# Turning the cross scores of a graph network's first phase on VectorE and GpSimd in place of TensorE

## The chip, the core and the metric

One core of a Trainium2 chip runs the whole program. Its engines are named as in the profile: PE is TensorE (matmuls), PEld its weight loads, DVE is VectorE, ACT is ScalarE, POOL is GpSimd, SP is the engine that issues the DMAs. Each works through its own queue in order and waits on semaphores. The metric is the device time of one execution in microseconds, the median over runs; lower is better.

## The reference

128 graphs of 64 nodes with 384 features pass through three graph layers. The first two follow each other after one normalisation, the third has a normalisation of its own; a sum with the earlier x closes each block. What a layer computes:

```python
h = jnp.maximum(_layernorm(x, axis=-1), 0.0)             # before layers 1 and 3

u = jnp.einsum('bid,bjd->bij', h, h) / temper            # temper = sqrt(384)
a = jax.nn.softmax(u, axis=-1)
delta = a * adjacency_matrix
attn = delta / (jnp.sum(delta, axis=-1, keepdims=True) + 1e-10)
hl = h @ wl.T + b_l
hs = h @ ws.T + b_s
hr = h @ wr.T + b_r
ctx = (attn * upper) @ hl + diag_a[..., None] * hs + (attn * lower) @ hr
o = (ctx - mean) / jnp.sqrt(var + LN_EPS) * g + beta
h = jax.nn.relu(o)
```

## The kernel before, in words

**Tiles.** Two graphs make a tile of 128 rows, so there are 64 tiles; a step works on two tiles (k = 0 and 1). A phase is one layer, 32 steps, so there are 96 steps (`Step.n`). The body of a step is written for each engine by hand, in the order in which the engine is to run it; a hardware loop (`walk`) repeats it in pairs, with the first two and last four steps of each phase written out. In the body for step s, PE projects and weighs the tiles of s while everything else prepares s+1 (`nxt`), up to the normalisation of s+4 (`fourth`).

**Precision.** PE multiplies rounded fp32 numbers. To keep fp32 accuracy each operand is split into a rounded part HI (made by ACT) and the rest LO (made by DVE), and a product is three matmuls: HI·HI, HI·LO, LO·HI. For the scores both operands are the same nodes, so LO·HI is the transpose of HI·LO. `scores` therefore makes, for each tile, 128 columns of HI·HI and 128 columns of HI·LO in one PSUM bank (`score_bank`, seen as `scores4` [row, tile, which of the two, column]). The second block is called the cross scores.

**The transposed part before.** ACT copies the cross scores of both tiles to SBUF (`copy_cross`, L548). PE multiplies each tile's copy by the identity (`turn_cross`, L426), which adds its transpose onto HI·HI in PSUM. DVE adds the copy itself (`sum_scores`, L744): two instructions, one for each half of the partitions, since of a tile of two graphs only the two 64x64 blocks on the diagonal are wanted. Then come the exponentials (ACT, L565), `mask_edges` (DVE, L773), `place_edges` (POOL, L989 and L993).

**The order of a step on PE.** Projection RIGHT of tile 0, `weigh` of the previous step's tile 1 (L475, six matmuls: three with the RIGHT side parts, then three with the LEFT ones), projection LEFT of tile 0, projection SELF of tile 0 (L442, nine matmuls each), `scores` of the next step (L418), projection RIGHT of tile 1, `turn_cross` of the next step, `weigh` of tile 0, projections LEFT and SELF of tile 1. I call the `weigh` of tile 1, which runs in the step after, the second `weigh`.

**What else the prediction names.** DVE: `split_nodes` (L727, the LO part of the next step's nodes), `context_stats` (L813), `split_side` (L808, the LO part of a projection), `turn_nodes` (L723, a transpose of 128x768 in 32x32 squares, for the tiles three steps ahead), `gather_input` (L710 and L711, mean and variance of the rows four steps ahead), `centre` (L832), `norm` (L841). ACT: `split_side` (L589), `fill_source` (L532), which waits for `split_nodes` on DVE. POOL: `input_rstd` (L977, L979), which waits for both `gather_input`, and `output_rstd` (L983).

```python
for side in (RIGHT, LEFT):
    pe.wait_ge(side_hi[side], s.tile(k) + 1)
    pe.wait_ge(side_lo[side], s.tile(k) + 1)
    for a, b in PASSES:
```

## Time and profile before

| | |
|---|---|
| median of 3 runs | 1239.68 us (1238.2 to 1240.05) |
| profiled execution | 1238.95 us |
| its span | 1237.2 us |
| PE busy | 98% |
| DVE busy | 88% |
| ACT busy | 67% |
| POOL busy | 26% |
| two products of `turn_cross` (L426) | 192 matmuls, 96 pairs, 32 of them in the first phase |

How to read the rows further down. A timeline row is: start in us, length in us, engine, line of the kernel, operation, tile written <- tiles read, shape, count; in brackets how long the engine was idle just before and what ended that. Instructions in one row are merged, so its length is that of all of them. Rows of one engine can overlap: an instruction may begin before the one ahead of it has fully ended. Matmul ends are modelled, so the distance between the starts of two PE rows says more than a length. A row of a stretch gives, for PE, PEld, DVE, ACT and POOL in this order, the busy time and the number of instructions, then the granted PE clock, the DMA share and GB/s. A row of a group is: line, engine, operation, tiles, shapes, count | busy us, mean ns of one | idle before it and what ended that.

### The profile page before, as it was taken

Reading aid. Unit: us, or ns where it says so; the run is one execution under the profiler, and the core shown is the slowest. Engines: PE = TensorE matmul, PEld = TensorE weight load, DVE = VectorE, ACT = ScalarE, POOL = GpSimd, SP = SyncE. Lnnn points to the kernel's source line nnn. Section 1 sums busy time; section 2 is a strip of 40 time slices with the busy share of each in tenths; the row PEclk is TensorE's granted clock in tenths of the full one; section 3 lists DMA queues with packets and bytes.
Section 4 is the critical chain, followed back from the end, with each engine's and each line's share of the span. In section 5 each row is a group of like instructions: output and inputs, shape, how many; then the busy total and the mean of one; then the engine's idle time right before and its main releaser. Section 6 shows DMA issues by size and latency. Waiting matters only on the chain.

```text
span 1237.2 us, 27493 instructions
## 1 busy us (share of the span) xinstructions
PE 1218.6 (98%) x7162; PEld 1209.0 (98%) x7162; DVE 1090.4 (88%) x3125; ACT 833.8 (67%) x2079; POOL 324.4 (26%) x438
## 2 busy tenths in 40 slices
PE   8899999999999999999999999999999999999997
PEld 6899999999999999999999999999999999999997
DVE  6888888888887889999999999999999999999986
ACT  5666666666667776666667666776666666666663
POOL 2322222222223321111212121342323232323221
PEclk9899999999999999999999999999999999999999
DMA  5423232323233333233333333432232323232321
GB/s 178 134 82 119 83 119 83 117 84 115 87 106 122 106 100 103 95 101 100 95 106 95 106 95 106 133 108 95 96 106 95 106 95 102 97 97 97 99 96 43
DMA packets 112899, 126.91 MB, mean 103 GB/s; under 512 B 11104, under 2 KB 100192, under 8 KB 112864
## 3 DMA queue, kind: packets, MB, share of 16 engines
q1 hardware_dynamic: 112864, 126.50, 32.7%
q8 instruction: 15, 0.25, 0.1%
q14 instruction: 20, 0.16, 0.0%
HBM read 76.91 MB, written 49.55 MB: 102 GB/s over the span
## 4 chain that ended last, share of the span: by engine, by line
PE 92%; DVE 4%; issue 3%; POOL 1%; ACT 0%; POOLq 0%; DVEq 0%; ACTq 0%
PE left_bank L442 23%; PE right_bank L442 23%; PE context_bank L442 23%; PE context_bank L475 16%; PE score_bank L418 5%; PE score_bank L426 1%; DVE node_t L727 1%; DVE context L841 0%; POOL weight L1000 0%; DVE weight L796 0%; DVE in_stats L706 0%; DVE turned L723 0%; DVE context L832 0%; PE right_bank L499 0%; DVE attn_t L801 0%
## 5 line engine op out<-in xcount | busy, mean ns | idle before, releaser
L442 PE MATMUL left_bank<-weight,node_t 128*128 128x384 f32 x1728 | 338.9, 339 | 0.3 <-DVE weight L796 0.3
L442 PE MATMUL context_bank<-weight,node_t 128*128 128x384 f32 x1728 | 333.1, 337 | 1.9 <-DVE weight L796 1.9
L442 PE MATMUL right_bank<-weight,node_t 128*128 128x384 f32 x1728 | 333.7, 337 | 0.6 <-ACT right_bank L583 0.6
L589 ACT ACTIVATE side_parts<-right_bank 128x384 fp32r<-128x384 f32 x192 | 94.4, 491 | 316.6 <-PE context_bank L475 316.6
L442 PEld LDWEIGHTS context_bank<-weight,node_t 128*128 128x128 f32 x1728 | 304.2, 189 | 2.4 <-issue 2.2
L442 PEld LDWEIGHTS left_bank<-weight,node_t 128*128 128x128 f32 x1728 | 305.3, 189 | 0.6 <-issue 0.6
L442 PEld LDWEIGHTS right_bank<-weight,node_t 128*128 128x128 f32 x1728 | 298.7, 188 | 1.4 <-issue 1.1
L475 PE MATMUL context_bank<-side_parts,attn_t 128*128 128x386 f32 x1152 | 241.5, 345 | 5.7 <-issue 5.4
L475 PEld LDWEIGHTS context_bank<-side_parts,attn_t 128*128 128x128 f32 x1152 | 199.8, 190 | 8.5 <-issue 7.5
L727 DVE TENSOR_TENSOR node_t<-nodes,node_t 128x768 fp32r<-128x768 f32 x94 | 120.4, 1281 | 17.7 <-ACT node_t L537 17.6
L993 POOL TENSOR_TENSOR edge_block<-edge,tri 128x512 f32<-128x512 f32 x96 | 133.7, 1393 | 0.0
L983 POOL TENSOR_TENSOR rstd<-spread,scalars 128x2 f32<-128x2 f32 x96 | 66.2, 689 | 257.0 <-DVE spread L824 257.0
L723 DVE STREAM_TRANSPOSE turned<-nodes 128x768 f32<-128x768 f32 x94 | 92.0, 979 | 45.7 <-ACT nodes L532 42.7
L601 ACT ACTIVATE context_bank<-context_bank,diag 128x386 f32<-128x386 f32 x192 | 105.1, 547 | 36.9 <-PE context_bank L442 36.1
L989 POOL TENSOR_TENSOR own_edge<-edge,tri 128x128 f32<-128x128 f32 x96 | 47.3, 493 | 302.7 <-DVE edge L773 302.7
L832 DVE SCALAR_TENSOR_TENSOR context<-context_bank,moments,vector_rows 128x384 f32<-128x384 f32 x192 | 117.1, 610 | 2.4
L813 DVE BATCH_NORM_STATS2 stats<-context_bank 128x6 f32<-128x384 f32 x192 | 107.3, 559 | 11.9 <-PE context_bank L475 11.9
L808 DVE TENSOR_TENSOR side_parts<-right_bank,side_parts 128x384 fp32r<-128x384 f32 x192 | 106.7, 556 | 10.9 <-ACT side_parts L589 7.0
L808 DVE TENSOR_TENSOR side_parts<-left_bank,side_parts 128x384 fp32r<-128x384 f32 x192 | 103.0, 536 | 1.6 <-ACT side_parts L589 1.6
L977 POOL TENSOR_TENSOR in_spread<-in_moments,scalars 128x2 f32<-128x2 f32 x64 | 17.3, 271 | 312.5 <-DVE in_moments L711 312.5
L595 ACT ACTIVATE context_bank<-vector_rows 128x386 f32<-128x386 f32 x192 | 94.5, 492 | 0.0
L583 ACT ACTIVATE left_bank<-vector_rows 128x384 f32<-128x384 f32 x192 | 93.7, 488 | 0.0
(75 smaller groups left out, 1521.5 us busy)
## 6 DMA issues: line engine op xcount, KB each, us to landing
squares<-turned SPq DMA_DIRECT2D x94, 384.0 KB, 2.7
nodes<-squares SPq DMA_DIRECT2D x376, 96.0 KB, 2.2
rows<-x SPq DMA_DIRECT2D x64, 384.0 KB, 3.6
out<-rows SPq DMA_DIRECT2D x31, 384.0 KB, 2.6
adj_in<-adj SPq DMA_DIRECT2D x96, 64.0 KB, 1.9
piece<-weights SPq DMA_DIRECT2D x18, 192.0 KB, 2.6
rows<-weights SPq DMA_DIRECT2D x3, 576.0 KB, 8.0
vector_rows<-vectors SPq DMA_DIRECT2D x3, 384.0 KB, 7.0
```

What stands on the lines that cost most here:

```text
L442: mm = nc.tensor.matmul(bank[:, 0:D], node_t[:, s.parity, k, c, a], weight[:, s.phase % 2, w, c, b], start=False, stop=(c, a) == (CH - 1, ...
L475: mm = nc.tensor.matmul(context_bank[k][:, 0:DX], attn_t[:, a, k, 1 - side], side_parts[:, side, b], start=False, stop=(side == LEFT and a ...
L583: nc.scalar.activation(side_bank[side][k][:, 0:D], vector_row(s.phase, ROW_LEFT + side), ACT.Copy)\
L589: nc.scalar.activation(side_parts[:, side, HI, 0:D], side_bank[side][k][:, 0:D], ACT.Copy).then_inc(side_hi[side], 1)
L595: nc.scalar.activation(context_bank[k][:, 0:DX], vector_row(s.phase, ROW_SELF, 2), ACT.Copy)\
L601: nc.scalar.activation(context_bank[k][:, 0:DX], context_bank[k][:, 0:DX], ACT.Identity, scale=diag[:, s.parity, k:k + 1]).then_inc(self_s ...
L723: nc.vector.transpose(turned[:, :, :], source_blocks).then_inc(nodes_turned, 1)
L727: nc.vector.tensor_tensor(node_rows(s, LO), moved_rows, node_rows(s, HI).bitcast(F32), ALU.subtract).then_inc(node_lo, 1)
L808: nc.vector.tensor_tensor(side_parts[:, side, LO, 0:D], side_bank[side][k][:, 0:D], side_parts[:, side, HI, 0:D].bitcast(F32), ALU.subtrac ...
L813: nc.vector.bn_stats(stats[:, k], context_bank[k][:, 0:D]).then_inc(stats_done, 1)
L832: nc.vector.scalar_tensor_tensor(context[:, k], context_bank[k][:, 0:D], moments[:, k, 0:1], vector_row(s.phase, ROW_GAMMA), ALU.subtract, ...
L993: nc.gpsimd.tensor_tensor(edge_block[:, :, :, :].rearrange("p k u (h j) -> p k (u h) j", h=2), edge[:, :, :].unsqueeze(2).to_broadcast([P, ...
```

## The change

Only steps of the first phase (n below 32) are treated in the new way (`squared`); in the other two phases the code does what it did.

- PE: the two products with the identity are gone, at the start as well.
- ACT: the copy of the cross scores is two instructions of 64 partitions, each only of the 64 columns for each tile that are wanted.
- DVE: `turn_cross` reads the cross scores in PSUM. Two transposes of 64x128 turn every 32x32 square in place; then, after a wait of DVE on its own result, four transposes of 32x64 write the off-diagonal squares of each 64x64 block over it, each to the neighbouring quarter of the partitions. They go to `own_edge`, a buffer that is free at that time.
- POOL: `add_cross` adds ACT's copy onto the turned squares.
- DVE: `sum_scores` waits for POOL and adds the result to HI·HI.

DVE, second step of the program (the body of a step, written out), from the input statistics to the second `norm`. Before:

```order
L706 BN_STATS in_stats<-rows 128x6 x2
L841 SCALAR_TENSOR_TENSOR rows<-context,rstd,vector_rows 128x384
L744 TENSOR_TENSOR score<-score_bank,cross 64x128 x2
L710 MEMSET scalars 128x1
L711 BN_AGGR in_moments<-in_stats 128x2
L710 MEMSET scalars 128x1
L711 BN_AGGR in_moments<-in_stats 128x2
L808 TENSOR_TENSOR side_parts<-right_bank,side_parts 128x384
L841 SCALAR_TENSOR_TENSOR rows<-context,rstd,vector_rows 128x384
```

The same place on DVE now; L866 is `norm`, L833 `split_side`, L770 the sum:

```order
L866 SCALAR_TENSOR_TENSOR rows<-context,rstd,vector_rows 128x384
L753 STREAM_TRANSPOSE own_edge<-score_bank 64x128 x2
L758 STREAM_TRANSPOSE own_edge<-score_bank 32x2x32 x4
L719 MEMSET scalars 128x1
L720 BN_AGGR in_moments<-in_stats 128x2
L719 MEMSET scalars 128x1
L720 BN_AGGR in_moments<-in_stats 128x2
L833 TENSOR_TENSOR side_parts<-right_bank,side_parts 128x384
L770 TENSOR_TENSOR score<-score_bank,own_edge 64x128 x2
L866 SCALAR_TENSOR_TENSOR rows<-context,rstd,vector_rows 128x384
```

Where the sum stood there are six transposes; the sum has moved behind both gathers and the RIGHT `split_side`.

POOL, the same step, from `output_rstd` to `place_edges`. Before:

```order
L983 TENSOR_TENSOR rstd<-spread,scalars 128x2
L977 TENSOR_TENSOR in_spread<-in_moments,scalars 128x2
L979 TENSOR_TENSOR in_rstd<-in_spread,scalars 128x2
L1000 TENSOR_TENSOR weight<-piece,weight 128x384 x2
L989 TENSOR_TENSOR own_edge<-edge,tri 128x128
```

The same place on POOL now; L1015 is the new addition:

```order
L1019 TENSOR_TENSOR rstd<-spread,scalars 128x2
L1008 TENSOR_TENSOR in_spread<-in_moments,scalars 128x2
L1010 TENSOR_TENSOR in_rstd<-in_spread,scalars 128x2
L1015 TENSOR_TENSOR own_edge<-own_edge,cross 128x128
L1036 TENSOR_TENSOR weight<-piece,weight 128x384 x2
L1025 TENSOR_TENSOR own_edge<-edge,tri 128x128
```

The addition stands behind the two operations of `input_rstd`, which need DVE's gathered moments.

```diff
@@ -70,6 +70,8 @@
         self.phase = self.n // PAIRS if isinstance(half, int) else phase
         self.g = self.n - PAIRS * self.phase
         self.bounded = self.phase != 1
+
+        self.squared = self.phase == 0
 
         self.normal = self.n - (PAIRS if self.phase == 2 else 0)
 
@@ -192,6 +194,8 @@
         first_bank = [edge_bank, score_bank]
         max_rows = edge_bank[:, 0:2 * NODES].rearrange("p (k i) -> p k i", k=2)
         score_copy = cross[:, :, 0:NODES]
+        cross_upper = cross[:, 0, :].rearrange("p (k j) -> p k j", k=2)
+        cross_lower = own_edge[:, :, :]
         scores4 = score_bank[:, :].rearrange("p (k a j) -> p k a j", k=2, a=2)
         source = nodes[:, :].rearrange("p (k d) -> p k d", k=2)
         source_blocks = nodes[:, :].rearrange("p (n q y) -> p q n y", q=QUARTERS, y=Q)
@@ -421,7 +428,7 @@
 
             def turn_cross(s):
 
-                pe.wait_ge(cross_copied, s.n + 1)
+                pe.wait_ge(cross_copied, 2 * s.n + 2)
                 for k in range(2):
                     mm = nc.tensor.matmul(score_bank[:, k * 256:k * 256 + P], cross[:, k], ident_r[:, :],
                                           start=False, stop=True, skip_group_check=True)
@@ -488,7 +495,7 @@
                 if nxt.exists():
                     scores(nxt)
                 project_side(s, 1, RIGHT)
-                if nxt.exists():
+                if nxt.exists() and not nxt.squared:
                     turn_cross(nxt)
                 weigh(s, 0)
                 project_side(s, 1, LEFT, within=(lambda: spread_max(nxt)) if nxt.exists() and not nxt.bounded else None)
@@ -509,8 +516,6 @@
             start = Step(0, 0, 0)
             transpose_first(start)
             scores(start)
-            open_bank(edge_bank)
-            turn_cross(start)
             walk(pe, body)
             weigh(Step(2, STEPS // 2 - 1, 1), 1)
 
@@ -545,7 +550,11 @@
             def copy_cross(s):
                 act.wait_ge(scored, s.n + 1)
                 at_least(act, score_summed, 2 * s.n)
-                nc.scalar.activation(cross[:, :, :], scores4[:, :, 1, :], ACT.Copy).then_inc(cross_copied, 1)
+                if not s.squared:
+                    nc.scalar.activation(cross[:, :, :], scores4[:, :, 1, :], ACT.Copy).then_inc(cross_copied, 2)
+                    return
+                for h, half in enumerate(HALVES):
+                    nc.scalar.activation(cross_upper[half], scores4[half, :, 1, h * NODES:(h + 1) * NODES], ACT.Copy).then_inc(cross_copied, 1)
 
             def totals(s):
                 act.wait_ge(max_bias_done, s.n + 1 - PAIRS)
@@ -737,13 +746,29 @@
                                                  node_t[:, s.parity, k, :, HI].bitcast(F32), ALU.subtract)
                 mm.then_inc(node_lo, 1)
 
+            def turn_cross(s):
+
+                dve.wait_ge(cross_copied, 2 * s.n + 2)
+                for h, half in enumerate(HALVES):
+                    mm = nc.vector.transpose(cross_lower[half], scores4[half, :, 1, h * NODES:(h + 1) * NODES])
+                mm.then_inc(squares_turned, 1)
+                dve.wait_ge(squares_turned, s.n + 1)
+                for q in range(QUARTERS):
+                    to, side, at = q ^ 1, q % 2, q // 2 * NODES
+                    mm = nc.vector.transpose(cross_lower[to * Q:(to + 1) * Q, :, side * Q:(side + 1) * Q],
+                                             scores4[q * Q:(q + 1) * Q, :, 1, at + (1 - side) * Q:at + (2 - side) * Q])
+                mm.then_inc(lower_turned, 1)
+
             def sum_scores(s):
 
-                dve.wait_ge(cross_turned, s.n + 1)
+                if s.squared:
+                    dve.wait_ge(cross_added, s.n + 1)
+                else:
+                    dve.wait_ge(cross_turned, s.n + 1 - PAIRS)
                 for h, half in enumerate(HALVES):
+                    other = cross_lower[half] if s.squared else cross[half, :, h * NODES:(h + 1) * NODES].bitcast(F32)
                     nc.vector.tensor_tensor(score[half], scores4[half, :, 0, h * NODES:(h + 1) * NODES],
-                                            cross[half, :, h * NODES:(h + 1) * NODES].bitcast(F32),
-                                            ALU.add).then_inc(score_summed, 1)
+                                            other, ALU.add).then_inc(score_summed, 1)
 
             def row_maximum(s):
 
@@ -863,8 +888,9 @@
                 split_side(s, 0, LEFT)
                 split_edges(s)
                 input_shift(second)
+                turn_cross(nxt)
+                turn_nodes(second)
                 sum_scores(nxt)
-                turn_nodes(second)
                 split_side(s, 1, RIGHT)
                 gather_stats(third)
                 context_stats(s, 0)
@@ -904,7 +930,9 @@
                     input_stats(fourth, 1)
                 if prev.exists():
                     norm(prev, 0)
-                if nxt.exists():
+                if nxt.exists() and nxt.squared:
+                    turn_cross(nxt)
+                if nxt.exists() and not nxt.squared:
                     sum_scores(nxt)
                 if nxt.exists() and not nxt.bounded:
                     row_maximum(nxt)
@@ -915,6 +943,8 @@
                 if prev.exists() and prev.phase > 0:
                     residual(prev, 0)
                 split_side(s, 1, RIGHT)
+                if nxt.exists() and nxt.squared:
+                    sum_scores(nxt)
                 if prev.exists():
                     norm(prev, 1)
                 context_stats(s, 0)
@@ -952,6 +982,7 @@
             input_shift(start.ahead(1))
             split_first(RIGHT)
             split_first(LEFT)
+            turn_cross(start)
             sum_scores(start)
             mask_edges(start)
             split_first(SELF)
@@ -978,6 +1009,11 @@
                 pool.wait_ge(in_spread_done, s.normal + 1)
                 nc.gpsimd.tensor_tensor(in_rstd[:, :], in_spread[:, :], minus_half[:, :], ALU.pow).then_inc(in_rstd_done, 1)
 
+            def add_cross(s):
+
+                pool.wait_ge(lower_turned, s.n + 1)
+                nc.gpsimd.tensor_tensor(cross_lower, cross_lower, cross_upper.bitcast(F32), ALU.add).then_inc(cross_added, 1)
+
             def output_rstd(s):
                 pool.wait_ge(spread_done, s.n + 1)
                 nc.gpsimd.tensor_tensor(rstd[:, :], spread[:, :], minus_half[:, :], ALU.pow).then_inc(rstd_done, 1)
@@ -1002,6 +1038,7 @@
 
             def first_step(s):
                 input_rstd(s.ahead(2))
+                add_cross(s.ahead(1))
                 input_rstd(s.ahead(3))
                 place_edges(s.ahead(1))
                 input_rstd(s.ahead(4))
@@ -1015,6 +1052,8 @@
                     output_rstd(prev)
                 if fourth.exists() and fourth.bounded:
                     input_rstd(fourth)
+                if nxt.exists() and nxt.squared:
+                    add_cross(nxt)
                 if len(pieces) > 0:
                     split_piece(*pieces[0])
                 if len(pieces) > 1:
@@ -1027,6 +1066,7 @@
             input_rstd(start)
             input_rstd(start.ahead(1))
             pool.wait_ge(triangles_in, 16)
+            add_cross(start)
             place_edges(start)
             walk(pool, body)
             output_rstd(Step(2, STEPS // 2 - 1, 1))
```

## Rows read from the trace of the kernel before

**Rows 1.** The page: busy time of the engines; chain that ended last.

```profile
PE 1218.6 (98%) x7162; PEld 1209.0 (98%) x7162; DVE 1090.4 (88%) x3125; ACT 833.8 (67%) x2079; POOL 324.4 (26%) x438
...
PE 92%; DVE 4%; issue 3%; POOL 1%; ACT 0%; POOLq 0%; DVEq 0%; ACTq 0%
```

**Rows 2.** Busy time of each engine from 100 to 399 us.

```profile
100.00:399.00 299.00, 299.00 (x1777) 299.00 (x1776) 248.69 (x754) 204.71 (x507) 79.60 (x119) 1.00 0.34 102
```

**Rows 3.** Timeline of PE, one step of the first phase.

```profile
212.11 1.21 PE L475 MATMUL context_bank<-side_parts,attn_t 128*128 128x386 f32 x6
213.16 1.74 PE L442 MATMUL left_bank<-weight,node_t 128*128 128x384 f32 x9
...
218.58 0.33 PE L426 MATMUL score_bank<-ident_r,cross 128*128 128x128 f32 x2
218.75 1.28 PE L475 MATMUL context_bank<-side_parts,attn_t 128*128 128x386 f32 x6
219.87 1.74 PE L442 MATMUL left_bank<-weight,node_t 128*128 128x384 f32 x9
...
224.57 0.68 PE L475 MATMUL context_bank<-side_parts,attn_t 128*128 128x386 f32 x3
```

**Rows 4.** Timeline of DVE, the same step.

```profile
210.77 0.55 DVE L808 TENSOR_TENSOR side_parts<-left_bank,side_parts 128x384 fp32r<-128x384 f32 x1
...
212.09 0.96 DVE L727 TENSOR_TENSOR node_t<-nodes,node_t 128x768 fp32r<-128x768 f32 x1 [0.58 <-ACT node_t L537]
213.35 0.57 DVE L813 BATCH_NORM_STATS2 stats<-context_bank 128x6 f32<-128x384 f32 x1 [0.30 <-PE context_bank L475]
...
215.65 0.98 DVE L723 STREAM_TRANSPOSE turned<-nodes 128x768 f32<-128x768 f32 x1 [0.75 <-ACT nodes L532]
...
219.56 0.60 DVE L744 TENSOR_TENSOR score<-score_bank,cross 64x128 f32<-64x128 f32 x2
220.22 0.06 DVE L710 MEMSET scalars<- 128x1 f32 x1
...
220.65 0.56 DVE L808 TENSOR_TENSOR side_parts<-right_bank,side_parts 128x384 fp32r<-128x384 f32 x1
221.13 0.61 DVE L841 SCALAR_TENSOR_TENSOR rows<-context,rstd,vector_rows 128x384 f32 x1
...
223.24 0.55 DVE L808 TENSOR_TENSOR side_parts<-left_bank,side_parts 128x384 fp32r<-128x384 f32 x1
```

**Rows 5.** Timeline of ACT, the same step.

```profile
213.41 0.49 ACT L589 ACTIVATE side_parts<-right_bank 128x384 fp32r<-128x384 f32 x1 [1.35 <-PE context_bank L475]
...
214.22 1.30 ACT L532 ACTIVATE nodes<-rows,in_shift,in_rstd 128x384 f32 x2
...
217.28 0.38 ACT L548 ACTIVATE cross<-score_bank 128x256 fp32r<-128x256 f32 x1
```

**Rows 6.** Timeline of POOL, the same step.

```profile
220.66 0.19 POOL L977 TENSOR_TENSOR in_spread<-in_moments,scalars 128x2 f32<-128x2 f32 x1 [4.99 <-DVE in_moments L711]
220.93 0.69 POOL L979 TENSOR_TENSOR in_rstd<-in_spread,scalars 128x2 f32<-128x2 f32 x1
222.55 0.47 POOL L989 TENSOR_TENSOR own_edge<-edge,tri 128x128 f32<-128x128 f32 x1 [0.92 <-DVE edge L773]
```

**Rows 7.** Groups of DVE by line and shape, whole kernel.

```profile
L808 DVE TENSOR_TENSOR side_parts<-right_bank,side_parts 128x384 fp32r<-128x384 f32 x192 | 106.7, 556 | 10.9 <-ACT side_parts L589 7.0
...
L744 DVE TENSOR_TENSOR score<-score_bank,cross 64x128 f32<-64x128 f32 x192 | 55.2, 287 | 14.3 <-PE score_bank L426 9.7
```

**Rows 8.** Timeline of DVE, then of PE, at the start.

```profile
15.19 0.60 DVE L744 TENSOR_TENSOR score<-score_bank,cross 64x128 f32<-64x128 f32 x2
...
19.83 3.19 PE L442 MATMUL context_bank<-weight,node_t 128*128 128x384 f32 x9 [1.95 <-DVE weight L796]
...
34.62 2.27 PE L475 MATMUL context_bank<-side_parts,attn_t 128*128 128x386 f32 x6 [3.15 <-issue]
```

**Rows 9.** Timeline of DVE in step 28.

```profile
382.73 0.56 DVE L808 TENSOR_TENSOR side_parts<-right_bank,side_parts 128x384 fp32r<-128x384 f32 x1 [1.09 <-ACT side_parts L589]
```

More of the change, by code:

```diff
@@ L236, in adj_gnn_program @@
         cross_turned = sem("cross_turned")
+        squares_turned = sem("squares_turned")
+        lower_turned = sem("lower_turned")
+        cross_added = sem("cross_added")
         score_summed = sem("score_summed")
```

## The prediction

> **What bounds the kernel now.** I read the engine totals and the chain of waits first: PE is busy for 98% of the span and holds 92% of the chain that ended last [rows 1]. The stretch from 100 to 399 us is the steady part of the first phase, which is the phase the change touches: PE is busy for 299.00 of its 299.00 us at full granted clock, DVE for 248.69, ACT for 204.71, POOL for 79.60 [rows 2]. So a microsecond taken from PE there is a microsecond of the kernel as long as no other engine comes to set the pace. One step (two tiles) is read between two second `weigh` groups: 224.57 - 212.11 = 12.46 us [rows 3].
>
> DVE has little room. In the step from 212.09 to 224.56 it is idle three times: 0.58 us for ACT's rounded nodes, 0.30 us for PE, 0.75 us for ACT's next source tiles, 1.63 us together, all early in the step; from 215.65 until its last `split_side` ends at 223.79 it waits for nobody [rows 4]. Its own work is thus 12.46 - 1.63 = 10.83 us a step. The place where PE would first feel a late DVE is the second `weigh`: its first three matmuls use the RIGHT parts, the last three the LEFT parts. The LEFT parts are ready at 210.77 + 0.55 = 211.32 [rows 4], the fourth matmul starts half-way between 212.11 and 213.16, at 212.64 [rows 3]. Margin 1.32 us.
>
> **What goes from PE.** Two products of 128 columns (`turn_cross`). They start at 218.58 and the next group at 218.75, 0.17 us; the `weigh` behind them takes 1.12 us to the next group, against 1.05 us for the one with no such pair ahead of it [rows 3]. So 0.17 + 0.07 = 0.24 us a step; a PE-bound step would be 12.22 us.
>
> The Trainium skill, "VectorE: DVE Perf Modes", section "The TRN2 errata", gives a matmul max(60, 6 + columns) cycles, 134 cycles or 56 ns for each of these, so an estimate of 0.11 us for the pair: by that rule even the full gain is less than half of what the rows show. The rows are used.
>
> **What DVE gets.** Six transposes out of PSUM, two of 64x128 and four of 32x64, with a wait of DVE on itself between them. I call their time T. The trace has one transpose, 128x768, 0.98 us [rows 4]. The cost of a column comes from two subtractions out of PSUM: (556 - 287) / (384 - 128) = 1.05 ns [rows 7]. So 128 columns would take 0.98 - 640 x 0.00105 = 0.307 us and 64 columns 0.240 us. Whether they overlap matters: neighbours on all 128 partitions start 0.48 us apart though the first takes 0.56 (220.65 and 221.13), but the two half-partition sums of 287 ns together fill 0.60 us, which is no overlap and a gap of about 0.03 [rows 4, 7]. The transposes change partitions each time as those sums do, so I take no overlap: T = 2 x 0.307 + 4 x 0.240 + 6 x 0.03 = 1.75 us. From below, with 0.08 us of overlap each and 0.10 for the self-wait: 2 x 0.227 + 4 x 0.160 + 0.10 = 1.19. From above, 0.08 us more than T for each, since no transpose from PSUM and none on 32 partitions is in the trace: about 2.4. Less than nothing is excluded: they are added instructions and DVE loses only the order of a sum.
>
> The same page and section give VectorE 120 + columns cycles out of PSUM: 258 ns and 192 ns, an estimate of 1.28 us for all six. The row of the 128-column sum, 287 ns, lies above that rule's 258 ns. By the rule the forecast below would be 0.47 us a step lower, about 1269 us.
>
> **What POOL gets, and the new wait.** One addition of 128x128; its neighbour is `own_edge`, 0.47 us [rows 6]. POOL is idle enough, but its queue matters: `add_cross` stands behind `input_rstd`, whose two operations wait for the moments that DVE gathers after its transposes. And `sum_scores` on DVE now waits for `add_cross`, with only one `split_side` (0.48 us start to start) left between. From the gather's start at 220.22: 0.44 to POOL's start (220.66), 0.27 to its second operation (220.93), 0.69 for that, 0.47 for the addition, 0.04 to wake DVE: 1.91 us until the sum can start [rows 4, 6]. DVE itself is there after 0.43 + 0.48 = 0.91. It stands idle for 1.00 us. Queued behind that wait on DVE are the second `norm`, the statistics, `mask_edges`, `centre` and the LEFT `split_side`, which PE waits for.
>
> ACT's copy becomes two of half the partitions and ends well before 219.56, when DVE would use it (now 217.28 + 0.38) [rows 4, 5]; nothing for that.
>
> **The new step.** The delay before the LEFT parts is T + about 1.0, 2.75 us, over the margin of 1.32 (less the 0.24 by which PE is earlier). So PE waits in `weigh`, and the step is the loop through that wait, counted from the end of the LEFT `split_side`:
> PE's fourth matmul wakes, an estimate of 0.05; 212.64 to ACT's `split_side` at 213.41, 0.77; to ACT's `fill_source` at 214.22, 0.81; to DVE's `turn_nodes` at 215.65, 1.43; to 219.56, where the transposes now start, 3.91 [rows 3 to 5]. Sum 6.97. Then T, 0.06 to the gather, 1.91 to the sum, 0.60 + 0.03 for the sum, and 2.66 from 221.13 to 223.79 for all that follows [rows 4]. Together 12.23 + T = 13.98 us, 1.52 more than 12.46. DVE's other path in this loop (diagonal, `split_nodes`, statistics, spread) has lost its idle 0.58 and 0.30 and arrives before ACT does, so it doesn't count. The first `weigh` needs edges that DVE splits ahead of the transposes, so these don't delay it.
>
> Steps 1 to 27 have `input_rstd` ahead of the addition (the tile four steps on is still in the first phase): 27 x 1.52 = 41.0. Steps 28 to 30 have none and less DVE work, and DVE even waits 1.09 us for ACT there [rows 9]: PE stays the bound, 3 x -0.24 = -0.7. The start: the sum at 15.19 waits for T, 0.04, 0.47 and 0.04 = 2.30 us, and what follows it on DVE is what PE waits for at 19.83 for 1.95 us [rows 8]: +2.3. Sum 41.0 - 0.7 + 2.3 = +42.6. The profiled execution took 1238.95 us (span 1237.2), so 1281.6; the median of the runs is 0.7 above it: 1282.
>
> With T = 1.19 it is 27 x 0.96 + 1.7 - 0.7 = +27, 1266; with 2.4, 27 x 2.17 + 3.0 - 0.7 = +61, 1300.
>
> **Rivals.**
> 1. POOL's queue costs nothing: the addition is done when DVE gets to the sum (POOL's `input_rstd` earlier or shorter than its rows). Then the loop is 13.98 - 1.00 = 12.98, +0.52 a step, +14, and +2 at the start: 1255. For it: POOL is idle for nearly 5 us before. Against it: that idle is a wait for DVE's moments, named in the row [rows 6], and DVE makes them after the transposes.
> 2. Faster: PE remains the bound and everything added disappears in DVE's 1.63 us of idle and the margin of 1.32. The place is the second `weigh`; it decides by T plus POOL's wait: the loop without both is 11.23 us, so together they must stay under 1.23 us to gain at all and under 0.99 for the whole gain of 31 x -0.24 = -7.4: 1232. For it: 2.95 us of idle and margin look like room for 2.75. Against it: the idle lies ahead of waits that come from PE through ACT, so it can't be used by work that is later in the step; and 0.99 is below even the lowest T.
> 3. The clock: PE will stand idle for about 1.7 us in each step. At the start of the trace a `weigh` took 2.27 us in place of 1.21 after an idle stretch of 3.15 us [rows 8, 3]. If one `weigh` a step went so, 27 x 1.06 = 29 us more: 1311. Against it: the granted clock is at full speed from 100 to 399 us [rows 2], and the idle stretches would be half as long as that one.
> 4. The sum is the same on another route, that is, DVE takes up all of it unseen and nothing measurable is left: 1240. It needs T + wait at 1.23 exactly, a narrow point.
>
> **Chances.** Forecast 0.80; rival 1 0.08; rival 2 0.06; rival 3 0.04; rival 4 0.02. The forecast's own range is 1266 to 1300. I reach down to rival 1 and leave out 2, 4 and the clock: 1254 to 1300. Within 0.2% is about what a measurement here can't tell from none. Faster 0.06, same 0.02, slower 0.92.
>
> **What would show it.** In the first phase after: steps of about 14.0 us from `weigh` to `weigh`; PE idle 1.5 to 2 us a step inside the second `weigh`, ended by DVE's LEFT `split_side`; DVE idle about 1.0 us before `sum_scores`, ended by POOL's addition; POOL's addition right behind `in_rstd`; six transposes in about 1.75 us; steps of 12.22 us at 28 to 30; the second and third phase unchanged. Wrong: PE at 100% from 100 to 399 us; a sum that starts without waiting; transposes well away from 0.31 and 0.24 us; a granted clock under 1.00 in the phase.

## The result: 5.5% slower, and the profile after

The changed kernel takes 1306.76 us (1305.15 to 1307.41, 4 runs), the kernel before 1239.59 us in the same comparison; the ratio is 1.0545 with a 95% interval of 1.0532 to 1.0557. The direction was forecast, the size was not: +67 us against +42, and the time lies above the stated range of 1254 to 1300.

In the new profile `project` is L449, `weigh` L482, `scores` L425, `seed_side` L592, the exponentials L574, the sum L770, the transposes L753 and L758, the addition L1015, `input_rstd` L1008 and L1010, ACT's `split_side` L598, `scale_self` L610.

First the page: engine totals, chain by engine, and the group of PE's RIGHT projections (columns as in [rows 7]).

```profile
PE 1235.3 (95%) x7096; PEld 1216.2 (93%) x7096; DVE 1145.0 (88%) x3317; ACT 840.3 (64%) x2111; POOL 337.4 (26%) x470
...
PE 60%; issue 24%; POOL 7%; DVE 6%; ACT 1%; POOLq 0%; DMA 0%; DVEq 0%; SPq 0%; ACTq 0%
...
L449 PE MATMUL right_bank<-weight,node_t 128*128 128x384 f32 x1728 | 344.1, 344 | 50.6 <-ACT right_bank L592 49.8
```

PE held 92% of the chain before [rows 1]. Now 50.6 us of idle time stand ahead of the RIGHT projections, and ACT's seed of the right bank ended nearly all of them. The forecast had the idle time in `weigh`, ended by DVE.

The stretch from 100 to 399 us, answering to rows 2:

```profile
100.00:399.00 299.00, 263.10 (x1454) 256.71 (x1454) 246.18 (x766) 174.84 (x443) 76.12 (x122) 0.96 0.28 84
```

PE has 35.9 us of idle time where it had none, and the granted clock is 0.96, no longer 1.00. Two things, then. PE's timeline shows both (answers to rows 3):

```profile
202.81 1.85 PE L449 MATMUL right_bank<-weight,node_t 128*128 128x384 f32 x9 [1.88 <-ACT right_bank L592]
204.50 1.21 PE L482 MATMUL context_bank<-side_parts,attn_t 128*128 128x386 f32 x6
...
217.20 2.34 PE L449 MATMUL right_bank<-weight,node_t 128*128 128x384 f32 x9 [1.88 <-ACT right_bank L592]
219.33 2.13 PE L482 MATMUL context_bank<-side_parts,attn_t 128*128 128x386 f32 x6
221.26 1.95 PE L449 MATMUL left_bank<-weight,node_t 128*128 128x384 f32 x9
```

From one RIGHT projection to the next, 217.20 - 202.81 = 14.39 us, with PE idle for 1.88 of them. The step that follows is a slow one: the same `weigh` takes 2.13 us instead of 1.21.

What PE waits for is found by going back. DVE, POOL and ACT in the same step (answers to rows 4, 6 and 5):

```profile
211.95 0.63 DVE L753 STREAM_TRANSPOSE own_edge<-score_bank 64x128 f32<-64x128 f32 x2
212.62 1.02 DVE L758 STREAM_TRANSPOSE own_edge<-score_bank 32x64 f32<-32x64 f32 x4
...
214.00 0.56 DVE L833 TENSOR_TENSOR side_parts<-right_bank,side_parts 128x384 fp32r<-128x384 f32 x1
215.46 0.61 DVE L770 TENSOR_TENSOR score<-score_bank,own_edge 64x128 f32<-64x128 f32 x2 [0.91 <-POOL own_edge L1015]
...
218.34 0.55 DVE L833 TENSOR_TENSOR side_parts<-left_bank,side_parts 128x384 fp32r<-128x384 f32 x1
```

```profile
214.04 0.20 POOL L1008 TENSOR_TENSOR in_spread<-in_moments,scalars 128x2 f32<-128x2 f32 x1 [5.99 <-DVE in_moments L720]
214.32 0.69 POOL L1010 TENSOR_TENSOR in_rstd<-in_spread,scalars 128x2 f32<-128x2 f32 x1
214.97 0.46 POOL L1015 TENSOR_TENSOR own_edge<-own_edge,cross 128x128 f32<-128x128 f32 x1
```

```profile
216.18 0.26 ACT L574 ACTIVATE score<-score 128x64 f32<-128x64 f32 x1 [3.02 <-DVE score L770]
...
216.68 0.47 ACT L592 ACTIVATE right_bank<-vector_rows 128x384 f32<-128x384 f32 x1
217.09 0.47 ACT L598 ACTIVATE side_parts<-left_bank 128x384 fp32r<-128x384 f32 x1
```

DVE's six transposes take 1.69 us, from 211.95 to 213.64. POOL's addition is behind its two input operations, and DVE stands idle for 0.91 us for it. ACT stands idle for 3.02 us for the sum, because the exponentials are the next entry of its queue. And behind the exponentials in that queue is the seed of the next RIGHT bank, which has nothing to do with the scores. It ends at 217.15; PE starts at 217.20.

The starts of `scores`, one in each step, give the steps one by one. In the 27 steps that the forecast counted (1 to 27), before took 12.47 us each (12.69 for the first), 336.9 in all; now 403.0. Ten of them lie between 15.9 and 16.6 us, the other seventeen average 14.29.

Taken step by step, the mean granted clock is 0.89 or 0.90 in each of the ten and 1.00 in each of the seventeen; in the step shown it is still 1.00 from 214.9 to 217.2 us, while PE stands idle, then 0.77 to 219.3, 0.50 to 221.3 (1.2 in place of 2.4 GHz), 0.87 to 223.0, and 1.00 again.

Steps 28 to 30 take 12.24, 12.36 and 12.64. The third `scores`, where this count begins, is 2.3 us later. Together +66.0, about 0 and +2.3, against +68.4 in the span (1305.6 and 1237.2).

### The profile page after: what moved, and what is told of

Read it like the earlier page. It is cut to its first block, busy times and chain, and to the rows that moved or that the text cites. A ratio compares the mean times of both kernels' runs of the same rounds, so it can differ in the third digit from the quotient of the medians.

```text
span 1305.6 us, 27721 instructions
## 1 busy us (share of the span) xinstructions
PE 1235.3 (95%) x7096; PEld 1216.2 (93%) x7096; DVE 1145.0 (88%) x3317; ACT 840.3 (64%) x2111; POOL 337.4 (26%) x470
## 4 chain that ended last, share of the span: by engine, by line
PE 60%; issue 24%; POOL 7%; DVE 6%; ACT 1%; POOLq 0%; DMA 0%; DVEq 0%; SPq 0%; ACTq 0%
PE right_bank L449 15%; PE left_bank L449 15%; PE context_bank L449 15%; PE context_bank L482 10%; PE score_bank L425 3%; POOL edge_block L1029 3%; POOL rstd L1019 1%; POOL in_rstd L1010 1%; POOL own_edge L1015 1%; POOL own_edge L1025 1%; PE score_bank L433 1%; DVE rows L866 1%; DVE node_t L736 1%; DVE score L770 1%; POOL in_spread L1008 0%
## 5 line engine op out<-in xcount | busy, mean ns | idle before, releaser
L449 PE MATMUL right_bank<-weight,node_t 128*128 128x384 f32 x1728 | 344.1, 344 | 50.6 <-ACT right_bank L592 49.8
L449 PEld LDWEIGHTS right_bank<-weight,node_t 128*128 128x128 f32 x1728 | 301.9, 191 | 60.7 <-ACT right_bank L592 55.8
L449 PE MATMUL left_bank<-weight,node_t 128*128 128x384 f32 x1728 | 340.9, 341 | 0.0
L449 PE MATMUL context_bank<-weight,node_t 128*128 128x384 f32 x1728 | 332.0, 337 | 3.5 <-DVE weight L821 3.1
L449 PEld LDWEIGHTS left_bank<-weight,node_t 128*128 128x128 f32 x1728 | 309.2, 191 | 0.0
L449 PEld LDWEIGHTS context_bank<-weight,node_t 128*128 128x128 f32 x1728 | 303.0, 188 | 4.0 <-issue 3.3
L598 ACT ACTIVATE side_parts<-right_bank 128x384 fp32r<-128x384 f32 x192 | 94.5, 492 | 302.8 <-PE context_bank L482 302.8
L482 PE MATMUL context_bank<-side_parts,attn_t 128*128 128x386 f32 x1152 | 248.1, 352 | 5.8 <-issue 5.5
L482 PEld LDWEIGHTS context_bank<-side_parts,attn_t 128*128 128x128 f32 x1152 | 209.3, 197 | 9.1 <-issue 7.9
L838 DVE BATCH_NORM_STATS2 stats<-context_bank 128x6 f32<-128x384 f32 x192 | 107.3, 559 | 16.9 <-PE context_bank L482 15.9
L610 ACT ACTIVATE context_bank<-context_bank,diag 128x386 f32<-128x386 f32 x192 | 104.8, 546 | 21.6 <-PE context_bank L449 21.2
L833 DVE TENSOR_TENSOR side_parts<-right_bank,side_parts 128x384 fp32r<-128x384 f32 x192 | 106.6, 555 | 7.1 <-ACT side_parts L598 4.4
L1008 POOL TENSOR_TENSOR in_spread<-in_moments,scalars 128x2 f32<-128x2 f32 x64 | 17.4, 271 | 337.1 <-DVE in_moments L720 337.1
L833 DVE TENSOR_TENSOR side_parts<-left_bank,side_parts 128x384 fp32r<-128x384 f32 x192 | 102.8, 535 | 1.6 <-ACT side_parts L598 1.6
L592 ACT ACTIVATE left_bank<-vector_rows 128x384 f32<-128x384 f32 x192 | 92.9, 484 | 0.0
```

What stands on the lines that cost most here:

```text
L449: mm = nc.tensor.matmul(bank[:, 0:D], node_t[:, s.parity, k, c, a], weight[:, s.phase % 2, w, c, b], start=False, stop=(c, a) == (CH - 1, ...
L482: mm = nc.tensor.matmul(context_bank[k][:, 0:DX], attn_t[:, a, k, 1 - side], side_parts[:, side, b], start=False, stop=(side == LEFT and a ...
L592: nc.scalar.activation(side_bank[side][k][:, 0:D], vector_row(s.phase, ROW_LEFT + side), ACT.Copy)\
L598: nc.scalar.activation(side_parts[:, side, HI, 0:D], side_bank[side][k][:, 0:D], ACT.Copy).then_inc(side_hi[side], 1)
L610: nc.scalar.activation(context_bank[k][:, 0:DX], context_bank[k][:, 0:DX], ACT.Identity, scale=diag[:, s.parity, k:k + 1]).then_inc(self_s ...
L833: nc.vector.tensor_tensor(side_parts[:, side, LO, 0:D], side_bank[side][k][:, 0:D], side_parts[:, side, HI, 0:D].bitcast(F32), ALU.subtrac ...
```

## Experiments

no_products is an edit of the kernel before, and act_swap_mid puts the code of act_swap into the kernel before for some of the steps; all others are edits of the changed kernel. Each comparison ran beside the kernel before (1239.1 to 1239.5 us). "Step" is the distance of `scores` starts in the steady part of the first phase.

| kernel | median, us | ratio to before, 95% | step, us | PE clock, 100 to 399 us |
|---|---|---|---|---|
| before | 1239.6 | | 12.47 | 1.00 |
| changed | 1306.76 | 1.0532 to 1.0557 | 14.29, ten at 15.9 to 16.6 | 0.96 |
| no_products | 1231.69 | 0.9924 to 0.9958 | 12.22 | 1.00 |
| seed_first | 1286.08 | 1.0361 to 1.0396 | 14.10 | 1.00 |
| add_first | 1268.67 | 1.0219 to 1.0253 | 13.38 | 1.00 |
| both | 1259.41 | 1.0145 to 1.0179 | 13.10 | 1.00 |
| both_two | 1234.79 | 0.9951 to 0.9978 | 12.22 | 1.00 |
| fill2 | 1298.47 | 1.0459 to 1.0498 | 14.38 | 1.00 |
| act_swap | 1239.50 | 0.9993 to 1.0011 | 12.22 | 1.00 |
| act_swap_mid | 1232.97 | 0.9933 to 0.9960 | 12.22 | 1.00 |

**no_products: what the two products cost.** From the kernel before:

```diff
-                if nxt.exists():
+                if nxt.exists() and not nxt.squared:      # squared: phase 0
                     turn_cross(nxt)
...
-            open_bank(edge_bank)
-            turn_cross(start)
```

> Leaves out part of the computation: in the first phase the transposed cross scores are not added at all; everything else is the kernel before. It measures what the two products cost on PE by themselves. If a product pair costs what the starts of the groups showed (0.24 us in a PE-bound step): steps of 12.22 us, 31 x 0.24 = 7.4 us less than before, 1232 us. If they hid behind weight loads or something else sets the step: no change, 1239.6 us. By the length of 128 columns at full clock alone (0.11 us the pair): 1236 us.

Measured 1231.69 us, 7.4 us less. PE's timeline, with the two `weigh` of a step, what follows each, and the next step's first:

```profile
202.78 1.21 PE L476 MATMUL context_bank<-side_parts,attn_t 128*128 128x386 f32 x6
203.83 1.74 PE L443 MATMUL left_bank<-weight,node_t 128*128 128x384 f32 x9
...
208.53 1.21 PE L476 MATMUL context_bank<-side_parts,attn_t 128*128 128x386 f32 x6
209.58 1.74 PE L443 MATMUL left_bank<-weight,node_t 128*128 128x384 f32 x9
...
215.00 1.21 PE L476 MATMUL context_bank<-side_parts,attn_t 128*128 128x386 f32 x6
```

215.00 - 202.78 = 12.22, and `weigh` takes 1.05 us to the next group here too, as in the step's other half. The reading from starts (0.17 + 0.07 = 0.24 us) held within 0.01: 12.47 became 12.22. With everything added at no cost the change would have brought these 7.4 us.

**seed_first: the seed ahead of the exponentials.**

```diff
                 seed_self(s, 1)
+                if nxt.exists() and nxt.squared:
+                    seed_side(nxt, 0, RIGHT)
                 if nxt.exists() and nxt.bounded:
                     exponentials(nxt)
...
-                if nxt.exists():
+                if nxt.exists() and not nxt.squared:
                     seed_side(nxt, 0, RIGHT)
                 split_side(s, 1, LEFT)
```

> The changed kernel, with ACT's seed of the next step's right bank issued ahead of the exponentials instead of behind them, in the first phase. Theory A (PE is held by that seed, which stands behind exponentials that wait for the sum): the idle time of 1.88 us ahead of the RIGHT projection goes, the step falls from 14.39 to the next loop, the one through the LEFT parts in the second weigh: 3.43 + 6.98 + 3.51 = 13.92 us. 27 x 0.47 = 13 us less, about 1294 us, with PE waiting inside weigh for DVE. Rival B (the LEFT parts already set the step and the seed is only the place where the wait is seen): no change, 1307 us. Rival C (most of the excess over the forecast is the lower PE clock after idle stretches and not the seed): the same idle at another place, clock drops stay, under 5 us less.

Measured 1286.08 us, 20.7 less than the changed kernel, where 13 were expected: 27 x (14.39 - 14.10) = 8 from the step, in place of 13, and another 13 from slow steps that are gone, which the expectation had left in. All its steps from 2 to 27 take 14.1 us. The idle time before RIGHT is gone and PE waits in the second `weigh`, as the forecast had it:

```profile
221.43 1.72 PE L449 MATMUL right_bank<-weight,node_t 128*128 128x384 f32 x9
224.33 0.79 PE L482 MATMUL context_bank<-side_parts,attn_t 128*128 128x386 f32 x3 [1.17 <-ACT context_bank L610]
225.32 0.77 PE L482 MATMUL context_bank<-side_parts,attn_t 128*128 128x386 f32 x3 [0.20 <-DVE side_parts L835]
```

It is two waits. The last three matmuls wait for DVE's LEFT parts, as forecast (by their starts, 225.92 - 224.33 = 1.59 us for a `weigh` that takes 1.05 elsewhere); the first three wait for ACT's `scale_self`, which is also behind the exponentials in ACT's queue. The step of 14.10 us stands against 13.98 forecast for this loop, and 13.92 when worked out again from the rows of after. Rival B falls: the seed was a wait of its own, and the longer one. Rival C had the clock as the larger part, which it was, but not that the drops would go with this idle time.

**add_first and both: POOL's addition ahead of its input operations.**

```diff
+                if nxt.exists() and nxt.squared:
+                    add_cross(nxt)
                 if fourth.exists() and fourth.bounded:
                     input_rstd(fourth)
-                if nxt.exists() and nxt.squared:
-                    add_cross(nxt)
```

> The changed kernel, with POOL's addition ahead of its two input operations. Theory A: DVE's wait before the sum (0.91 us) goes, the loop through sum, exponentials and seed is 14.39 - 0.91 = 13.48 us: 27 x 0.91 = 25 us less, about 1282 us; if with the shorter idle stretches PE keeps its full clock, up to 15 us less on top, 1267 us. Rival B (the loop through the LEFT parts sets the step): 13.92 - 0.91 = 13.01 us, 1269 us before any gain in clock. Rival D (POOL's order doesn't matter): 1307 us.

> Both edits together: the seed ahead of the exponentials, the addition ahead of POOL's input operations. Theory A: the step is 13.92 - 0.91 = 13.01 us, PE idle about 0.8 us a step; 27 x 0.55 = 15 us more than before plus 2.5 at the start, about 1256 us if PE's clock holds, up to 1270 if it still falls as in the changed kernel. Six transposes alone (1.7 us) are then what is left, so the kernel stays slower than 1239.6. A rival in which DVE's own work hides in its former idle time once the two queues are right: 12.22 us a step, 1233 us.

add_first: 1268.67 us, step 13.38. Theory A with the clock kept (1267) and rival B (1269) can't be told apart by the time; the step can tell, 13.38 against 13.48 and 13.01, and so can the wait. POOL's order was worth 1.01 us a step, close to the 1.00 of the forecast, and PE still waits for the seed:

```profile
214.48 1.85 PE L449 MATMUL right_bank<-weight,node_t 128*128 128x384 f32 x9 [0.88 <-ACT right_bank L592]
```

both: 1259.41 us where 1256 were expected, step 13.10 against 13.01. PE's waits have shrunk and lie in `weigh`:

```profile
211.84 0.80 PE L482 MATMUL context_bank<-side_parts,attn_t 128*128 128x386 f32 x3 [0.17 <-ACT context_bank L610]
212.83 0.77 PE L482 MATMUL context_bank<-side_parts,attn_t 128*128 128x386 f32 x3 [0.19 <-DVE side_parts L835]
```

**both_two: fewer transposes.** As both, without the four transposes of 32x64:

```diff
                 mm.then_inc(squares_turned, 1)
                 dve.wait_ge(squares_turned, s.n + 1)
-                for q in range(QUARTERS):
-                    to, side, at = q ^ 1, q % 2, q // 2 * NODES
-                    mm = nc.vector.transpose(...)
                 mm.then_inc(lower_turned, 1)
```

> The kernel with both queue edits, in addition without the four transposes of 32x64 (the off-diagonal squares of the transposed part are left as the first two instructions leave them, so that part of the sum is not the reference's). Theory A (with the queues right, the transposes on DVE are what is left): DVE gets 1.05 us less, the loop falls from 13.10 to 12.05, under PE's 12.22, and the steps are 12.22 us: 27 x 0.88 = 24 us less than with both edits, about 1235 us. Rival (the number of handovers between engines, not DVE's time, sets the loop): 13.1 us a step, 1259 us.

Measured 1234.79 us, and PE has no idle time from 60 to 430 us:

```profile
60.00:430.00 370.00, 370.00 (x2183) 370.00 (x2182) 334.75 (x1001) 264.46 (x676) 114.93 (x179) 1.00 0.34 103
```

So with both queues in order what is left of the loss is DVE's time for the transposes (its wait on itself, which goes with the four, included), not the handovers between engines, which are the same in number here.

**fill2: the clock.** The changed kernel with work for PE in its idle time:

```diff
                 project_self(s, 1)
+                if nxt.exists() and nxt.squared:
+                    for i in range(9):
+                        nc.tensor.matmul(edge_bank[:, 0:D], ident_r[:, :],
+                                         weight[:, s.phase % 2, SELF, i % CH, HI],
+                                         start=True, stop=True, skip_group_check=True)
```

> The changed kernel with nine more matmuls of 128x384 a step on PE, right behind the last projection of each step of the first phase; they multiply the identity by weights and their result goes to a bank that nothing reads there. They take 1.57 us of the 1.88 us in which PE otherwise stands idle before the RIGHT projection. Theory A (what lies above 14.39 us a step is PE at the lower granted clock after idle stretches): all steps at 14.39 us or the 14.1 us at which some stand now, no low stretch between 60 and 440 us, about 12 us less: 1294 us, though PE has more to do. Rival (the slow steps come from something else): 1307 us. Rival (PE has no room): 27 x 1.57 = 42 us more, 1349 us.

Measured 1298.47 us. (One of its four executions took 2507.84 us; why is open. The ratio leaves it out; without it the median is 1298.18.) PE has 9 more matmuls in each of 31 steps, and the kernel is 8.3 us faster. From 60 to 430 us, fill2 and then the changed kernel:

```profile
60.00:430.00 370.00, 361.36 (x2081) 353.09 (x2082) 312.95 (x980) 221.35 (x565) 96.39 (x155) 1.00 0.29 87
```

```profile
60.00:430.00 370.00, 324.94 (x1779) 316.97 (x1780) 303.03 (x945) 213.74 (x545) 92.30 (x149) 0.95 0.28 84
```

```profile
209.69 1.72 PE L505 MATMUL edge_bank<-weight,ident_r 128*128 128x384 f32 x9
211.74 1.83 PE L449 MATMUL right_bank<-weight,node_t 128*128 128x384 f32 x9 [0.33 <-ACT right_bank L596]
```

All steady steps are at 14.38 to 14.40 us; none is slow. The added work costs 4.1 us in steps 28 to 30, where PE is the bound (41.35 us for the three against 37.24), and 1.0 us ahead of step 1. The expectation of 12 us less had left both out. The 27 steps between take 389.2 us in place of 403.0. So the lower clock cost the changed kernel about 14 us. The other way to the same number: 27 x 14.39 is 388.5; 14.4 us are left.

**act_swap: ACT swaps the squares, DVE transposes once, nobody waits.** A transpose of 64x64 is a swap of the off-diagonal 32x32 squares and then a transpose within each square. Here ACT does the swap while it copies (the edit of the changed kernel in short form, waits and the first step left out):

```diff
 # ACT, behind the seed of the LEFT bank
+for h, half in enumerate(HALVES):
+    nc.scalar.activation(straight[half], scores4[half, :, 1, h * NODES:(h + 1) * NODES], ACT.Copy)
+for q in range(QUARTERS):
+    here, to, side, at = slice(q * Q, (q + 1) * Q), q ^ 1, q % 2, q // 2 * NODES
+    nc.scalar.activation(swapped[here, :, side * Q:(side + 1) * Q],
+                         scores4[here, :, 1, at + side * Q:at + (side + 1) * Q], ACT.Copy)
+    nc.scalar.activation(swapped[to * Q:(to + 1) * Q, :, side * Q:(side + 1) * Q],
+                         scores4[here, :, 1, at + (1 - side) * Q:at + (2 - side) * Q], ACT.Copy)
 # DVE, behind gather_input
-sum_scores: wait for cross_added; score = HI.HI + own_edge
+sum_scores: wait for the copies;  score = HI.HI + straight
+nc.vector.transpose(own_edge, swapped)
 # POOL, ahead of input_rstd
-own_edge = own_edge + cross_upper
+score = score + own_edge                # ACT's exponentials wait for this
 # ACT: seed_side(nxt, 0, RIGHT) ahead of the exponentials, as in seed_first
```

> A version without PE's products and without DVE's wait: ACT copies the cross scores twice, once straight (2 instructions) and once with the off-diagonal 32x32 squares swapped (8 instructions of 32x64), behind its seed of the LEFT bank; DVE makes the sum where it did, then one transpose of 128x128 from SBUF; POOL adds that onto the score, ahead of its input operations, and ACT's exponentials wait for POOL; the seed of the next RIGHT bank stands ahead of the exponentials. Theory A: DVE gets 0.31 us instead of 1.72 and no wait, the loop is 13.01 - 1.4 = 11.6 us, below PE's 12.22: PE sets the step, 31 x 0.24 = 7.4 us less than before, 1233 us with about 1 us lost at the start. Rival: ACT's extra 1.8 us make its split_side or the sum late and the step is 12.5 to 13 us: 1240 to 1254 us.

Measured 1239.50 us, the same as before within 0.1%. The steady step is PE's 12.22 us, as theory A had it, but 1233 us were expected. The last of ACT's ten copies, DVE's sum and transpose, POOL's addition and the exponentials:

```profile
209.91 0.22 ACT L567 ACTIVATE cross<-score_bank 32x64 fp32r<-32x64 f32 x1
210.16 0.49 ACT L613 ACTIVATE side_parts<-right_bank 128x384 fp32r<-128x384 f32 x1
...
211.95 0.26 ACT L589 ACTIVATE score<-score 128x64 f32<-128x64 f32 x1 [0.51 <-POOL score L1028]
```

```profile
210.35 0.61 DVE L783 TENSOR_TENSOR score<-score_bank,cross 64x128 f32<-64x128 f32 x2 [0.36 <-ACT cross L567]
210.99 0.31 DVE L771 STREAM_TRANSPOSE own_edge<-cross 128x128 f32<-128x128 f32 x1
```

```profile
211.38 0.46 POOL L1028 TENSOR_TENSOR score<-score,own_edge 128x128 f32<-128x128 f32 x1 [5.59 <-DVE own_edge L771]
```

The gain is given back at the two ends of the phase. The distances of `scores` at the start are 14.29, 20.42, 13.24 and 12.83 us where before had 11.27, 18.71, 12.69 and 12.47, together 5.6 more: the ten copies stand in ACT's queue ahead of work that the start waits for (DVE waits 2.80 us for ACT's part of the weights where it waited 0.69, and 1.87 us for the last copy before the second sum). The three steps of 12.47 before the second phase became 12.62, 13.00 and 12.99.

**act_swap_mid: the same, only for the scores of steps 3 to 28.** Against act_swap, shortened (the counts of some waits change with it):

```diff
-        self.squared = self.phase == 0
+        self.squared = self.phase == 0 and (not isinstance(self.n, int) or 3 <= self.n <= PAIRS - 4)
```

> The version with ACT's swapped copy, used only for the scores of steps 3 to 28; steps 0 to 2 and 29 to 31 use PE's products as before. With the swapped copy in all steps the steady steps were 12.22 us but the first four and the last three together took about 6 us more than before. Theory A: 26 steps with 0.24 us less and nothing lost at the ends: 6.3 us less than before, 1233 us. Rival: the loss moves with the changeover (ACT's queue takes a step or two to settle): 1236 to 1239 us.

Measured 1232.97 us where 1233 were expected, ratio 0.9947 (0.9933 to 0.9960): half a per cent faster than before. The distances at the start are 10.61, 19.04, 13.08, then 12.22 to the end of the stretch and 12.48, 12.47, 12.47 for the last three. Its stretch of 299 us:

```profile
100.00:399.00 299.00, 299.00 (x1766) 299.00 (x1765) 263.30 (x788) 250.28 (x714) 95.22 (x143) 1.00 0.34 103
```

PE is at 299.00 of 299.00 again. DVE has 263 us instead of 249 and ACT 250 instead of 205 [rows 2]: the work went mostly to the engine that had the room.

## Why the prediction was off, point by point

**PE's part, right.** 0.24 us a step: 12.22 us in the four kernels in which PE is the bound. The estimate of 0.11 us from the Trainium skill ("VectorE: DVE Perf Modes", section "The TRN2 errata") would have given 3.5 us; the removal brought 7.4.

**T, right.** 1.75 us forecast, 1.69 measured, 310 ns for 64x128 and 246 ns for 32x64 where 307 and 240 were worked out. No overlap between neighbours on different partitions, as taken from the two half-partition sums. The same section's 120 + columns, an estimate of 1.28 us, was low again.

**POOL's wait, right.** 1.00 us forecast, 0.91 seen; taking it away gave 1.01 us a step (14.39 to 13.38).

**The end pieces, right.** +2.3 us at the start as forecast, though 0.24 of it lies ahead of the first `scores`, which this change doesn't touch and which starts anywhere from 11.0 to 12.5 us in the ten profiles: 2.0 us belong to the change. Steps 28 to 30 average 12.4 us instead of 12.22.

**The loop, wrong.** The step that failed: "So PE waits in `weigh`, and the step is the loop through that wait". Behind the wait on DVE the forecast listed what is queued on DVE. It did not list what is queued on ACT behind the exponentials, which wait for that same sum: the seed of the next RIGHT bank and `scale_self`. The seed made the loop 14.39 us. The loop of the forecast exists and is the next one: seed_first uncovered it at 14.10 against 13.98.

The seed's loop can be worked out from the rows of before like the other:

```profile
207.09 0.60 DVE L744 TENSOR_TENSOR score<-score_bank,cross 64x128 f32<-64x128 f32 x2
```

```profile
208.47 0.25 ACT L565 ACTIVATE score<-score 128x64 f32<-128x64 f32 x1
...
208.94 0.48 ACT L583 ACTIVATE right_bank<-vector_rows 128x384 f32<-128x384 f32 x1
```

```profile
210.54 1.73 PE L442 MATMUL right_bank<-weight,node_t 128*128 128x384 f32 x9
```

From PE's RIGHT projection at 210.54 to the fourth matmul of `weigh` at 212.64 are 2.10 us, from there to the transposes 6.92, to the sum T + 0.06 + 1.91 = 3.72, the sum 0.60, from the start of the exponentials to the end of the seed 209.42 - 208.47 = 0.95. With 0.11 from the sum to the exponentials and 0.05 from the seed to PE, both read in the new profile, the estimate is 14.45 us. The margins alone don't show it: the seed's room (1.12 us ahead of PE, and 0.78 between the sum and the exponentials) is larger than the 1.32 us of the LEFT parts. But the sum is late by 3.72 us and the LEFT parts only by 2.75, because the sum was also moved behind the gathers and the RIGHT `split_side`.

The loop's share of the miss is 27 x (14.39 - 13.98) = 11 us: 8 for the seed (down to the 14.10 of seed_first) and 3 because the forecast's own loop is 0.12 us longer than its sum. Which term of that sum was short is open.

**The clock, wrong.** Rival 3 was named, priced at one slow `weigh` a step and given 0.04, on the ground that the idle stretches would be half as long as the one at the start. They were 1.88 us, and in ten of 27 steps PE ran partly at 1.2 instead of 2.4 GHz: such a step took about 1.55 us more, and the whole cost about 14 us, by the steps and by fill2. Why these ten and not the others is open. seed_first, with idle time of 1.17 and 0.20 us a step in place of 1.88, had no slow steady step, and add_first, with 0.88, had none. The two misses together, 25 us, are the whole of what was missing (42.6 + 25 = 67.6, against 67 to 68). The stated range had no room for either: its upper end of 1300 came from a longer T alone, and T was right.

**The rivals.** Rival 1 (POOL's queue costs nothing) and 4 are out. Rival 2 (the additions disappear in idle time) didn't happen, but its point of decision exists and lies near where it was put, at 0.99 us of added DVE time: both_two adds 0.63 us and act_swap 0.31, and both run at 12.22 us in the steady part, while `both` adds 1.69 and runs 0.88 above it. From `both` an estimate of the point is 1.69 - 0.88 = 0.8 us.

## What to carry to other kernels

When an added wait makes a result late, list what stands behind every engine's wait for that result, not only behind the first: a trivial copy that is queued behind can be what the bound engine needs next. Work taken from a saturated engine has to land where there is margin in the loop, not where there is idle time in the sum: DVE had 2 us idle a step (rows 2) and by the estimate above could take about 0.8. And a stall on the bound engine can cost more than its length: here 1.88 us of idle time a step also brought PE's clock down in ten steps, for 14 us in all. Such a cost belongs in the forecast as a term. And when a change moves an instruction down its own queue, count its lateness from the new place, not from what was added ahead of it.

## What the runs showed of the hardware that was not expected

- A pair of 128-column products costs PE 0.24 us between groups of 384 columns, twice what 256 columns cost in those groups (nine matmuls of 384 in 1.57 us, so 0.12): taking the pair out of 31 steps gave 7.4 us.
- More work made the kernel faster: 279 matmuls of 128x384 in PE's idle time kept the granted clock at 1.00 and saved 8.3 us.
- A partition-crossing copy of 32x64 on ACT out of PSUM takes 0.21 us, its neighbour starts 0.23 us later; a DVE transpose of 128x128 in SBUF takes 0.31 us, as long as one of 64x128 out of PSUM. Four of 32x64, which turn half as many elements as the 128x128, take 1.02 us.
